# The last expert of a post-norm decoder layer: statistics of the final rows earlier, their normalisation on one engine, one bank per slot tile

## Chip, cores and metric

The kernel runs on one core of one Trainium2 chip. The number judged is the device time of one execution in microseconds. Three runs of the kernel before took 1951.0, 1952.97 and 1957.52 us (median 1952.97).

## What is computed

One decoder layer with layer norm after each of three parts: linear attention, cross attention, and a mixture of experts. Only the third is touched by the change. Cut to that:

```python
logits = xf @ router_w + router_b                 # 2048 tokens, 8 experts
topk_p, topk_i = top_k(softmax(logits), 2)        # two experts per token, weights renormalised
# each expert has cap = 640 slots; tokens are put into slots in order of expert
h  = gelu(einsum('ecd,edf->ecf', buf, w1) + b1[:, None, :])      # 512 -> 1024
eo = einsum('ecf,efd->ecd', h, w2) + b2[:, None, :]              # 1024 -> 512
out = zeros_like(xf).at[st].add(eo_flat[slot] * w)
x = _layernorm(x + out)                            # (x - mean) / sqrt(var + 1e-5), no scale, no shift
```

All is float32. Each large product is made of three products of rounded parts (high x high, high x low, low x high), which is why operands are split into `_hi` and `_lo`.

## The kernel before

The program is one plan, a list of stages written by `do(stage, ...)`; each engine walks the same list and runs the stages that it has a function for. So the order of `do` calls is the order of work on every engine, and an instruction that waits holds all that stands behind it on its engine. Engines hand work over by semaphores (`wait_ge`, `then_inc`); `step.settle` makes VectorE or GpSimd wait for its own last instruction before the next.

Experts go one after another. For expert `e`, `up(e, f)` for f = 0 to 7 computes 128 of the 1024 hidden columns for 640 slots (24 pairs of products of 320 columns on TensorE, line 1440); ScalarE applies the Gelu (line 2077) and makes the high part (line 2082); VectorE makes the low part `hid_lo` (line 1826). A hidden buffer is used by every second f, so the Gelu of f waits for the low part of f - 2. Behind the first four f, ScalarE and VectorE also split the second weights (`split_w2`, line 1821). Then `down(e, i)` for i = 0 to 4 multiplies 128 slots by the second weights (24 products of 512 columns, line 1167, into one PSUM bank). VectorE adds the bias and the router's weight, and GpSimd adds the rows into `y_rows` in HBM, which started as a copy of the input of this part.

The last expert (e = 7) is different. When all rows of the other seven experts lie in `y_rows`, `fetch_y(q)` loads all 2048 rows back in eight pieces of 256 rows (two tiles of 128 each, 512 KB, issued by SyncE), and `gather_y` gathers the 640 rows that belong to the last expert's slots into the five tiles `xg`. Rows without a slot of the last expert are final and only need their layer norm: `final_stats(q)` takes mean and variance on VectorE (line 1869), behind every fourth piece it starts the inverse root, `final_root(half)` ends it on GpSimd with three Newton steps, and the rows are normalised and stored. This is done for all 2048 rows. Rows with a slot of the last expert are done in `finish(7, i)`: product, bias, weight, sum with the gathered row, statistics, inverse root by three Newton steps on one value per partition, normalisation. `scatter` (GpSimd) then writes them over the rows stored before; it waits until all stores of the final rows have landed (`out_done`).

In the kernel before, the eight pieces of final rows are shared: `final_act` takes pieces 0, 1, 4 and 5 on ScalarE, which also issues their stores, `final_dve` takes pieces 2, 3, 6 and 7 on VectorE (line 1885), stored by SyncE. The statistics of pieces 0 to 3 stand behind f = 4 to 7 of the last expert, those of pieces 4 and 5 ahead of `finish(7, 0)` and those of 6 and 7 ahead of `finish(7, 1)`. The products of `finish` use two PSUM banks in turn (6 and 7): TensorE may write a bank again when VectorE has added the bias from it (line 1849).

Of the kernel before, what the change touches and what calls it, by code (L numbers as in the profile page):

```python
# [30 lines left out]
NF = F // P  # L31
# [9 lines left out]
RSQRT_MAGIC = 0x5F3759DF  # L41
PASSES = 3
# [18 lines left out]
HALF_Y = B * NT // 2  # L61

# [63 lines left out]
def program(nc, t):  # L126
    ctx = ExitStack()
    with ctx:
# [183 lines left out]
        def chunk_of(b, mc):  # L312
# [72 lines left out]
        final_act, final_dve = signal("final_act"), signal("final_dve")  # L385
        out_done = signals("out_done", 2, 16)
# [78 lines left out]
            "finish": lambda e, i: (down_summed, eo_biased, slot_ready),  # L465
# [5 lines left out]
            "final_act": lambda q: (final_act, out_done[0]),  # L471
            "final_dve": lambda q: (final_dve, out_done[1]),
# [7 lines left out]
            "fold_turn": folded, "parts": parts_copied, "logits": logits_done, "ranks": ranks_taken, "finish": eo_biased,  # L480
# [563 lines left out]
        def normalise(half):  # L1044
            for q in range(PIECES_Y // 4):
                do("final_act", half * PIECES_Y // 2 + q)
                do("final_dve", half * PIECES_Y // 2 + PIECES_Y // 4 + q)

        for e in range(E):
# [23 lines left out]
            fetch("fetch_w1", e + 2)  # L1073
        for i in range(NS):
            if i < 2:
                for q in range(PIECES_Y // 4):
# [396 lines left out]
        def _(_eng):  # L1473
# [368 lines left out]
            def finish(e, i):  # L1842
                turn = e * NS + i
                out, row, a, b, y = eo[turn % EO], xg[i][:, :], slot_a[:, i:i + 1], slot_b[:, i:i + 1], slot_y[:, i:i + 1]
                dve.wait_ge(*down_summed[e, i])
                dve.wait_ge(*b2_in[e % 2][e])
                if i < EO:
                    dve.wait_ge(*y_added[down_order[turn - EO]])
                V.tensor_tensor(out[:, :], bank(bank_of["finish", e, i]), b2s[e % 2][:, :], ALU.add) \  # L1849
                    .then_inc(eo_biased.sem, 1)  # L1850
                dve.wait_ge(*eo_biased[e, i])
                dve.wait_ge(*xg_in[i][E, i])
# [3 lines left out]
                step.settle(V.tensor_scalar(a, mean_var_s[:, i, 1:2], EPS, None, ALU.add))  # L1856
                step.settle(V.tensor_scalar(y.bitcast(I32), a.bitcast(I32), 1, None, ALU.logical_shift_right))
                step.settle(V.tensor_scalar(y.bitcast(I32), y.bitcast(I32), -1.0, float(RSQRT_MAGIC),
                                            ALU.mult, ALU.add))
# [626 lines left out]
```

## Time and profile before

| | |
|---|---|
| median of 3 runs | 1952.97 us (1951.0 to 1957.52) |
| the profiled execution, its own time | 1955.99 us |
| its span | 1954.2 us, 26706 instructions |
| TensorE / VectorE / ScalarE / GpSimd busy | 97% / 64% / 45% / 42% of the span |
| chain that ended last, by engine | PE 82%, DVE 13%, DMA 2%, the rest 1% or less each |

In the rows below PE is TensorE's matmul, PEld its weight load, DVE is VectorE, ACT is ScalarE, POOL is GpSimd and SP is SyncE; a q behind a name means the queue that issues DMAs. Times are us from the span's start. The chain is followed back from the last instruction, at each step to what released it. A matmul's duration overlaps that of the next one, so their pitch is read from the starts.

### The profile page before, as it was taken

The numbers are of one execution on the slowest core, as the hardware profiler recorded it, in microseconds if no ns is written. First come the engines' busy times: TensorE is split into PE (matmuls) and PEld (weight loads), VectorE is DVE, ScalarE is ACT, GpSimd is POOL, SyncE is SP. The second block draws the span as 40 slices with busy tenths as digits, with TensorE's granted clock in tenths as the row PEclk, the third lists the DMA queues.
The fourth block names the chain that finished last, engine by engine and source line by source line (L and its number), as shares of the span: only waits on it lengthen the run. The fifth ranks groups of instructions, "written<-read, shape, count | busy, mean of one in ns | idle before, by whom it ended". The sixth has DMA issues, their size and how long they took to land.

```text
span 1954.2 us, 26706 instructions
## 1 busy us (share of the span) xinstructions
PE 1886.4 (97%) x10016; PEld 1281.6 (66%) x10016; DVE 1254.8 (64%) x2391; ACT 888.0 (45%) x1595; POOL 822.1 (42%) x740
## 2 busy tenths in 40 slices
PE   8999999989999999999999999999969999999996
PEld 6887677777655555555445545544439998899995
DVE  5675573257778788888678778777653444344457
ACT  3312322222566666666456456546724433344431
POOL 3002201100388788888567657665011223222132
PEclk9999999999999999999999999999978999999998
DMA  7003524573667476757434424421234444434453
GB/s 275 22 1 114 189 87 165 193 208 124 172 132 178 101 182 134 170 120 156 98 103 104 109 59 131 109 65 62 82 111 138 135 125 119 128 99 125 135 140 113
DMA packets 123777, 244.87 MB, mean 125 GB/s; under 512 B 11232, under 2 KB 29424, under 8 KB 119600
## 3 DMA queue, kind: packets, MB, share of 16 engines
q1 hardware_dynamic: 108608, 185.46, 32.0%
q0 software_dynamic: 13952, 55.61, 13.9%
q10 hardware_dynamic: 1088, 2.10, 0.3%
q8 instruction: 79, 1.29, 0.3%
q14 instruction: 50, 0.41, 0.1%
HBM read 148.46 MB, written 62.42 MB: 108 GB/s over the span
## 4 chain that ended last, share of the span: by engine, by line
PE 82%; DVE 13%; DMA 2%; issue 1%; ACT 1%; SPq 1%; POOL 1%; POOLq 0%; DVEq 0%; ACTq 0%
PE banks L1167 34%; PE banks L1440 12%; PE banks L1347 11%; PE banks L1317 10%; PE banks L1336 8%; DVE max L1638 8%; PE banks L1368 4%; PE banks L1173 2%; DMA k_parts<-out_lo 1%; DMA k_half<-in_xwk_t 0%; PE banks L1249 0%; DMA raw<-in_wk_t 0%; DVE stats_y L1869 0%; DVE den_c L1657 0%; POOL x_nat L2148 0%
## 5 line engine op out<-in xcount | busy, mean ns | idle before, releaser
L1638 DVE TENSOR_REDUCE max<-banks 128x1 f32<-128x512 f32 x1024 | 627.1, 680 | 144.3 <-PE banks L1317 143.4
L2137 POOL TENSOR_TENSOR probs<-probs,probs 128x512 f32<-128x512 f32 x464 | 583.0, 1291 | 249.0 <-PE banks L1347 249.0
L2017 ACT ACTIVATE probs<-banks 128x512 f32<-128x512 f32 x1024 | 520.2, 607 | 260.7 <-PE banks L1336 260.1
L1317 PE MATMUL banks<-k_stack,q_stack 98*128 98x512 f32 x1024 | 428.3, 425 | 4.0 <-DVE max L1638 2.7
L1336 PE MATMUL banks<-q_stack,k_stack 98*128 98x512 f32 x1024 | 377.1, 398 | 2.6 <-ACT probs L2017 2.6
L1317 PEld LDWEIGHTS banks<-k_stack,q_stack 98*128 98x128 f32 x1024 | 192.2, 188 | 194.5 <-DVE max L1638 106.2
L1347 PE MATMUL banks<-probs,v_grp 128*32 128x512 f32 x2048 | 251.7, 604 | 0.0
L1336 PEld LDWEIGHTS banks<-q_stack,k_stack 98*128 98x128 f32 x1024 | 191.7, 188 | 62.3 <-ACT probs L2017 17.8
L2184 POOL DMA_INDIRECT y_rows<-eo,tok x35 | 71.4, 2040 | 170.3 <-DVE eo L1839 116.1
L1826 DVE TENSOR_TENSOR hid_lo<-hid,hid_hi 128x640 fp32r<-128x640 f32 x64 | 52.8, 825 | 139.0 <-ACT hid_hi L2082 139.0
L1167 PE MATMUL banks<-w_hi,hid_hi 128*128 128x512 f32 x320 | 129.6, 405 | 2.3 <-DVE eo L1849 2.2
L1347 PEld LDWEIGHTS banks<-probs,v_grp 128*32 128x32 f32 x2048 | 60.2, 109 | 109.1 <-issue 103.0
L2148 POOL TENSOR_TENSOR x_nat<-x_nat,bxo_row 128x512 f32<-128x512 f32 x16 | 21.3, 1360 | 252.3 <-PE banks L1173 252.3
L1167 PE MATMUL banks<-w_hi,hid_lo 128*128 128x512 f32 x320 | 126.8, 396 | 0.0
L1167 PE MATMUL banks<-w_lo,hid_hi 128*128 128x512 f32 x320 | 126.3, 395 | 0.0
L1440 PE MATMUL banks<-xe_hi,w_hi 128*128 128x320 f32 x512 | 117.8, 312 | 1.5 <-issue 1.5
L1440 PE MATMUL banks<-xe_lo,w_hi 128*128 128x320 f32 x512 | 117.8, 311 | 0.0
L1440 PE MATMUL banks<-xe_hi,w_lo 128*128 128x320 f32 x512 | 117.6, 311 | 0.0
L2077 ACT ACTIVATE hid<-banks,b1c 128x640 f32<-128x640 f32 x64 | 51.0, 796 | 137.0 <-PE banks L1440 136.0
L2175 POOL DMA_INDIRECT xg<-x_rows,tok x40 | 39.5, 988 | 167.5 <-PE banks L1173 134.2
L1368 PE MATMUL banks<-probs,ones 128*32 128x512 f32 x784 | 105.7, 601 | 1.5 <-DVE probs L1652 0.8
L1836 DVE TENSOR_TENSOR eo<-banks,b2s 128x512 f32<-128x512 f32 x35 | 24.2, 692 | 106.1 <-PE banks L1167 106.1
(263 smaller groups left out, 2806.7 us busy)
## 6 DMA issues: line engine op xcount, KB each, us to landing
k_stack<-k_parts SPq DMA_DIRECT2D x144, 256.0 KB, 5.3
w_raw<-in_L_ffn_w SPq DMA_DIRECT2D x16, 2048.0 KB, 8.4
probs<-probs POOLq DMA_DIRECT2D x31, 1024.0 KB, 10.1
q_stack<-q_parts SPq DMA_DIRECT2D x48, 256.0 KB
v_grp<-v_rows SPq DMA_DIRECT2D x48, 256.0 KB, 3.3
raw<-in_ctx_t SPq DMA_DIRECT2D x8, 1024.0 KB, 7.1
k_parts<-out_hi SPq DMA_DIRECT2D x32, 256.0 KB, 2.5
k_parts<-out_lo SPq DMA_DIRECT2D x32, 256.0 KB, 2.9
```

The source lines that it names most:

```text
L1167: done = nc.tensor.matmul(out, lhsT, rhs, start=start and n == 0, stop=stop and n == len(operands) - 1)
L1317: nc.tensor.matmul(out, queries_of(t)[:, j, tile_of(k)], keys_of(t)[0:STK + SHIFT, j, mc * HALF:(mc + 1) * HALF], start=True, stop=True) \
L1336: nc.tensor.matmul(out, keys_of(t)[0:STK + SHIFT, j, tile_of(s)], queries_of(t)[:, j, :], start=True, stop=True).then_inc(scored.sem, 1)
L1347: done = nc.tensor.matmul(bank(NUM)[j * DH:(j + 1) * DH, :], v_grp[:, s, j * DH:(j + 1) * DH], probs_of(t, s)[:, j, :], start=s == 0, stop ...
L1368: done = nc.tensor.matmul(bank(DEN)[j * DH:(j + 1) * DH, :], ones[:, 0:DH], tile[:, j, :], start=begun, stop=s == MT - 1 and tile is tiles ...
L1440: done = nc.tensor.matmul(pairs[first][:, h, 0:HC], w, x[:, h * HC:(h + 1) * HC], start=n == 0, stop=n == len(terms) - 1)
L1638: V.reduce_max(max4[:, tiles_of(t), :, :][:, k, j, mc:mc + 1], bank(bank_of["max", t, mc, k, j]), AX.X) \
L1826: V.tensor_tensor(hid_lo[:, f, :], hid[f % 2][:, :], hid_hi[:, f, :].bitcast(F32), ALU.subtract) \
L2017: S.activation(probs_of(t, s)[:, j, :], bank(bank_of["score", t, s, j]), ACT.Exp, scale=SCALE) \
L2077: S.activation(hid[f % 2][:, :].rearrange("p (h n) -> p h n", h=2), pairs[first][:, :, 0:HC], ACT.Gelu, bias=b1c[:, e, f:f + 1]).then_inc( ...
L2137: G.tensor_tensor(a[:, j, :], a[:, j, :], b[:, j, :], ALU.add).then_inc(pair_added.sem, 1)
L2184: G.indirect_dma_start(out=y_rows, in_=eo[turn % EO][:, :], in_offset=None, compute_op=ALU.add, out_offset=bass.IndirectOffsetOnAxis(ap=to ...
```

## The change

`STATS_AT` puts the statistics of the eight pieces behind f = 2 (piece 0), 3 (1), 4 (2, 3), 5 (4, 5) and 6 (6, 7) of the last expert. Both `final_root` and then all eight `final_act` follow the last `up`. `final_dve` is gone: ScalarE normalises all pieces, and SyncE issues all eight stores. The products of the five `finish` stages go to five different banks (6, 7, 4, 5, 0). The bias of the second product is no longer added to the product but to the gathered row, times the slot's weight, in a new stage `bias_slot(i)`, which stands one tile ahead of the `finish` that uses it; so `finish` has one full-width instruction fewer. The Newton iteration of `finish` is written with half the variance, so that a step has two instructions and not three, and one instruction ahead of it falls away (`finish` had 18 instructions and has 13; with `bias_slot` it is 14 per slot tile).

```diff
+HALF_MAGIC = RSQRT_MAGIC - 0x400000 - 2 ** 31
+STATS_AT = {2: (0,), 3: (1,), 4: (2, 3), 5: (4, 5), 6: (6, 7)}
+FINISH_BANKS = (6, 7, 4, 5, 0)
...
-                elif last:
-                    do("final_stats", f - NF // 2)
+                if last:
+                    for q in STATS_AT.get(f, ()):
+                        do("final_stats", q)
             if last:
                 do("final_root", 0)
+                do("final_root", 1)
+                for q in range(PIECES_Y):
+                    do("final_act", q)
                 break
...
+        finish_ring = Ring(*FINISH_BANKS)
+        do("bias_slot", 0)
         for i in range(NS):
-            if i < 2:
-                for q in range(PIECES_Y // 4):
-                    do("final_stats", PIECES_Y // 2 + i * PIECES_Y // 4 + q)
-            if i == 1:
-                do("final_root", 1)
-                normalise(0)
-            if i == 2:
-                normalise(1)
-            do("finish", E - 1, i, ring=down_ring)
+            do("finish", E - 1, i, ring=finish_ring)
+            if i + 1 < NS:
+                do("bias_slot", i + 1)
...
-                V.tensor_tensor(out[:, :], bank(bank_of["finish", e, i]), b2s[e % 2][:, :], ALU.add) \
-                    .then_inc(eo_biased.sem, 1)
-                step.settle(V.scalar_tensor_tensor(row, out[:, :], table[:, 1, turn:turn + 1], row, ALU.mult, ALU.add))
+                step.settle(V.scalar_tensor_tensor(row, bank(bank_of["finish", e, i]), table[:, 1, turn:turn + 1], row,
+                                                   ALU.mult, ALU.add))
...
-                step.settle(V.tensor_scalar(a, a, -0.5, None, ALU.mult))
                 for _ in range(3):
-                    root_step(a, b, y)
+                    step.settle(V.scalar_tensor_tensor(b, y, a, y, ALU.mult, ALU.mult))
+                    step.settle(V.scalar_tensor_tensor(y, b, 1.5, y, ALU.subtract, ALU.mult))
                 V.tensor_scalar(row, row, mean_var_s[:, i, 0:1], y, ALU.subtract, ALU.mult).then_inc(slot_ready.sem, 1)
+            def bias_slot(i):
+                turn = (E - 1) * NS + i
+                row = xg[i][:, :]
+                dve.wait_ge(*b2_in[(E - 1) % 2][E - 1])
+                dve.wait_ge(*xg_in[i][E, i])
+                step.settle(V.scalar_tensor_tensor(row, b2s[(E - 1) % 2][:, :], table[:, 1, turn:turn + 1], row,
+                                                   ALU.mult, ALU.add))
...
-            def final_dve_rows(q):
-                dve.wait_ge(*final_root[q // (PIECES_Y // 2)])
-                for n in range(q * TILES_Y, (q + 1) * TILES_Y):
-                    done = V.tensor_scalar(tile_y(n), tile_y(n), mean_var_y[:, n, 0:1], root_y[:, n:n + 1],
-                                           ALU.subtract, ALU.mult)
-                done.then_inc(final_dve.sem, 1)
...
                 done.then_inc(final_act.sem, 1)
-                act.wait_ge(*final_act[q])
-                S.dma_start(out_rows(q), piece_y(q)).then_inc(out_done[0].sem, 16)
...
-            def final_dve_rows(q):
-                sp.wait_ge(*final_dve[q])
-                Q.dma_start(out_rows(q), piece_y(q)).then_inc(out_done[1].sem, 16)
+            def final_act_rows(q):
+                sp.wait_ge(*final_act[q])
+                Q.dma_start(out_rows(q), piece_y(q)).then_inc(out_done.sem, 16)
```

On VectorE, in the last expert from the low part of f = 2 on, the kernel before has (`hid_lo` is the low part, `w_lo` the split of the second weights, `stats_y` the statistics of a piece, `yf_in0` the landing of piece 0):

```order
L1826 TENSOR_TENSOR hid_lo<-hid_173,hid_hi 128x640 [waits hid_split_hi]
L1821 TENSOR_TENSOR w_lo<-w_raw,w_hi 128x1024 [waits experts_hi]
L1826 TENSOR_TENSOR hid_lo<-hid_174,hid_hi 128x640 [waits hid_split_hi]
L1821 TENSOR_TENSOR w_lo<-w_raw,w_hi 128x1024 [waits experts_hi]
L1826 TENSOR_TENSOR hid_lo<-hid_173,hid_hi 128x640 [waits hid_split_hi]
L1869 BN_STATS stats_y<-y_final_191 128x6 [waits yf_in0]
```

and the changed kernel, from the same low part on:

```order
L1826 TENSOR_TENSOR hid_lo<-hid_173,hid_hi 128x640 [waits hid_split_hi]
L1821 TENSOR_TENSOR w_lo<-w_raw,w_hi 128x1024 [waits experts_hi]
L1871 BN_STATS stats_y<-y_final_191 128x6 [waits yf_in0]
L1871 BN_STATS stats_y<-y_final_191 128x6
L1874 BN_AGGR mean_var_y<-stats_y 128x2 [waits dve_step]
L1874 BN_AGGR mean_var_y<-stats_y 128x2
L1826 TENSOR_TENSOR hid_lo<-hid_174,hid_hi 128x640 [waits hid_split_hi]
L1821 TENSOR_TENSOR w_lo<-w_raw,w_hi 128x1024 [waits experts_hi]
L1871 BN_STATS stats_y<-y_final_191 128x6 [waits yf_in1]
```

The statistics of piece 0 moved from behind the low part of f = 4 to ahead of that of f = 3; the other pieces follow, and all eight stand ahead of the low part of f = 7.

On VectorE, in the last slot tile (i = 4) of the kernel before, with the three Newton steps cut to one:

```order
L1849 TENSOR_TENSOR eo_175<-banks,b2s_179 128x512 [waits down_summed]
L1853 SCALAR_TENSOR_TENSOR xg_168<-eo_175,table,xg_168 128x512 [waits xg_in4,eo_done]
L1854 BN_STATS stats_s<-xg_168 128x6 [waits dve_step]
L1855 BN_AGGR mean_var_s<-stats_s 128x2 [waits dve_step]
L1856 TENSOR_SCALAR slot_a<-mean_var_s 128x1 [waits dve_step]
L1857 TENSOR_SCALAR slot_y<-slot_a 128x1 [waits dve_step]
L1858 TENSOR_SCALAR slot_y<-slot_y 128x1 [waits dve_step]
L1860 TENSOR_SCALAR slot_a<-slot_a 128x1 [waits dve_step]
L1592 TENSOR_TENSOR slot_b<-slot_y 128x1 [waits dve_step]
L1593 TENSOR_TENSOR slot_b<-slot_b,slot_a 128x1 [waits dve_step]
L1594 SCALAR_TENSOR_TENSOR slot_y<-slot_b,slot_y 128x1 [waits dve_step]
```

and of the changed kernel:

```order
L1864 SCALAR_TENSOR_TENSOR xg_168<-b2s_179,table,xg_168 128x512 [waits xg_in4]
L1846 SCALAR_TENSOR_TENSOR xg_168<-banks,table,xg_168 128x512 [waits down_summed,dve_step]
L1848 BN_STATS stats_s<-xg_168 128x6 [waits dve_step]
L1849 BN_AGGR mean_var_s<-stats_s 128x2 [waits dve_step]
L1850 TENSOR_SCALAR slot_a<-mean_var_s 128x1 [waits dve_step]
L1851 TENSOR_SCALAR slot_y<-slot_a 128x1 [waits dve_step]
L1852 TENSOR_SCALAR slot_y<-slot_y 128x1 [waits dve_step]
L1855 SCALAR_TENSOR_TENSOR slot_b<-slot_y,slot_a 128x1 [waits dve_step]
L1856 SCALAR_TENSOR_TENSOR slot_y<-slot_b,slot_y 128x1 [waits dve_step]
```

The wait for the product (`down_summed`) has moved from the first full-width instruction to the second; one full-width instruction is left behind it ahead of the statistics, and a Newton step is two instructions. Between the slot tiles nothing else stands on VectorE any more. TensorE has the same instructions in the same order in both kernels; only the banks of the last three slot tiles differ.

## Rows read from the trace of the kernel before

**Rows 1.** Chain of waits, 1850 to 1955 us: shares by engine and line.
```profile
by line: PE banks L1440 26.8%; PE banks L1167 26.5%; DVE stats_y L1869 5.7%; issue 5.0%; DVE xg L1853 3.6%; DVE stats_s L1854 3.4%; DVE eo L1849 3.1%; DVE y_final L1885 2.9%; DVE slot_b L1593 2.5%; DVE slot_b L1592 2.4%; DVE slot_y L1594 2.
```

**Rows 2.** Windows: stretch, length, busy us of PE, PEld, DVE, ACT, POOL, granted clock, DMA.
```profile
1910.00:1920.00 10.00, 10.00 (x45) 8.15 (x44) 9.20 (x34) 2.35 (x4) 3.71 (x15) 1.00 0.04 14
1920.00:1930.00 10.00, 7.75 (x28) 5.89 (x27) 9.38 (x30) 1.00 (x2) 4.41 (x15) 0.83 0.53 198
```

**Rows 3.** Timeline of PE in the last expert's second products: start, us, what.
```profile
1907.43 0.39 PE L1167 MATMUL banks<-w_hi,hid_hi 128*128 128x512 f32 x1
...
1912.28 0.40 PE L1167 MATMUL banks<-w_hi,hid_hi 128*128 128x512 f32 x1
...
1923.85 0.39 PE L1167 MATMUL banks<-w_hi,hid_lo 128*128 128x512 f32 x1
1926.49 0.80 PE L1167 MATMUL banks<-w_hi,hid_hi 128*128 128x512 f32 x1 [2.25 <-DVE eo L1849]
...
1929.64 0.41 PE L1167 MATMUL banks<-w_lo,hid_hi 128*128 128x512 f32 x1
...
1939.19 0.40 PE L1167 MATMUL banks<-w_hi,hid_lo 128*128 128x512 f32 x1
```

**Rows 4.** Timeline of DVE, the last slot tile.
```profile
1943.87 0.68 DVE L1849 TENSOR_TENSOR eo<-banks,b2s 128x512 f32<-128x512 f32 x1
1944.59 0.75 DVE L1853 SCALAR_TENSOR_TENSOR xg<-eo,table,xg 128x512 f32<-128x512 f32 x1
...
1946.88 0.15 DVE L1860 TENSOR_SCALAR slot_a<-slot_a 128x1 f32<-128x1 f32 x1
1947.07 0.16 DVE L1592 TENSOR_TENSOR slot_b<-slot_y 128x1 f32<-128x1 f32 x1
...
1948.82 0.55 DVE L1863 TENSOR_SCALAR xg<-xg,mean_var_s,slot_y 128x512 f32<-128x512 f32 x1
```

**Rows 5.** Timeline of DVE beside the last expert's first products.
```profile
1891.63 0.82 DVE L1826 TENSOR_TENSOR hid_lo<-hid,hid_hi 128x640 fp32r<-128x640 f32 x1 [1.35 <-ACT hid_hi L2082]
1892.58 1.23 DVE L1821 TENSOR_TENSOR w_lo<-w_raw,w_hi 128x1024 fp32r<-128x1024 f32 x1
1895.15 0.83 DVE L1826 TENSOR_TENSOR hid_lo<-hid,hid_hi 128x640 fp32r<-128x640 f32 x1 [1.35 <-ACT hid_hi L2082]
...
1899.41 1.28 DVE L1869 BATCH_NORM_STATS2 stats_y<-y_final 128x6 f32<-128x512 f32 x2
...
1909.23 0.83 DVE L1826 TENSOR_TENSOR hid_lo<-hid,hid_hi 128x640 fp32r<-128x640 f32 x1 [1.21 <-ACT hid_hi L2082]
1909.97 1.28 DVE L1869 BATCH_NORM_STATS2 stats_y<-y_final 128x6 f32<-128x512 f32 x2
...
1912.06 1.28 DVE L1869 BATCH_NORM_STATS2 stats_y<-y_final 128x6 f32<-128x512 f32 x2
...
1913.54 1.25 DVE L1869 BATCH_NORM_STATS2 stats_y<-y_final 128x6 f32<-128x512 f32 x2
```

**Rows 6.** Issues, 1880 to 1955 (last: landing), and L2420 (fetch of the pieces).
```profile
out<-y_final SPq DMA_DIRECT2D x4, 512.0 KB, 3.4
...
L2420 SPq DMA_DIRECT2D y_final<-y_rows x8: 367/474/1312, 1886.1 to 1889.7; - x8
...
DMA to landing us min/median/max: 5.0/10.8/14.0
```

**Rows 7.** Timeline of POOL: first and last instruction of a root, last scatter.
```profile
1924.10 0.46 POOL L2217 TENSOR_SCALAR final_a<-final_a 128x8 f32<-128x8 f32 x1 [6.99 <-DVE final_y L1879]
...
1929.42 0.24 POOL L2221 TENSOR_SCALAR final_shift<-final_b 128x8 f32<-128x8 f32 x1
...
1950.15 0.97 POOL L2201 DMA_INDIRECT out<-xg,tok  x1 [3.97 <-DVE xg L1863]
```

**Rows 8.** Timeline of ACT: normalisation of one piece.
```profile
1917.15 1.52 ACT L2087 ACTIVATE y_final<-y_final,final_shift,final_y 128x512 f32<-128x512 f32 x2 [7.95 <-POOL final_shift L2221]
```

More of the change, by code:

```diff
@@ L384, in program @@
         final_stats, final_root = signal("final_stats"), signal("final_root")
-        final_act, final_dve = signal("final_act"), signal("final_dve")
-        out_done = signals("out_done", 2, 16)
+        final_act = signal("final_act")
+        out_done = signal("out_done", 16)
         dve_step, pool_step = (ctx.enter_context(nc.semaphore(n)) for n in ("dve_step", "pool_step"))
@@ L464, in program @@
             "down": lambda e, i: (down_summed, eo_biased, eo_ready, y_added),
-            "finish": lambda e, i: (down_summed, eo_biased, slot_ready),
+            "finish": lambda e, i: (down_summed, slot_ready),
             "scatter": lambda e, i: (slot_out,),
@@ L470, in program @@
             "final_root": lambda half: (final_root,),
-            "final_act": lambda q: (final_act, out_done[0]),
-            "final_dve": lambda q: (final_dve, out_done[1]),
+            "final_act": lambda q: (final_act, out_done),
         }
@@ L479, in program @@
             "score": exp_done, "num": num_copied, "den": den_copied, "rows": xo_added, "fold": fold_copied,
[L480 removed]
+            "fold_turn": folded, "parts": parts_copied, "logits": logits_done, "ranks": ranks_taken, "finish": slot_ready,
             "table": table_added, "x1_logits": part_hi, "turn_xe": xe_split, "up": hid_done, "down": eo_biased,
@@ L1843, in finish @@
                 turn = e * NS + i
-                out, row, a, b, y = eo[turn % EO], xg[i][:, :], slot_a[:, i:i + 1], slot_b[:, i:i + 1], slot_y[:, i:i + 1]
+                row, a, b, y = xg[i][:, :], slot_a[:, i:i + 1], slot_b[:, i:i + 1], slot_y[:, i:i + 1]
                 dve.wait_ge(*down_summed[e, i])
-                dve.wait_ge(*b2_in[e % 2][e])
-                if i < EO:
-                    dve.wait_ge(*y_added[down_order[turn - EO]])
-                V.tensor_tensor(out[:, :], bank(bank_of["finish", e, i]), b2s[e % 2][:, :], ALU.add) \
-                    .then_inc(eo_biased.sem, 1)
@@ L1851, in finish @@
-                dve.wait_ge(*eo_biased[e, i])
-                dve.wait_ge(*xg_in[i][E, i])
-                step.settle(V.scalar_tensor_tensor(row, out[:, :], table[:, 1, turn:turn + 1], row, ALU.mult, ALU.add))
+                step.settle(V.scalar_tensor_tensor(row, bank(bank_of["finish", e, i]), table[:, 1, turn:turn + 1], row,
+                                                   ALU.mult, ALU.add))
                 step.settle(V.bn_stats(stats_s[:, i, :], row))
                 step.settle(V.bn_aggr(mean_var_s[:, i, :], stats_s[:, i, :]))
-                step.settle(V.tensor_scalar(a, mean_var_s[:, i, 1:2], EPS, None, ALU.add))
+                step.settle(V.tensor_scalar(a, mean_var_s[:, i, 1:2], EPS, 0.5, ALU.add, ALU.mult))
@@ L1857, in finish @@
                 step.settle(V.tensor_scalar(y.bitcast(I32), a.bitcast(I32), 1, None, ALU.logical_shift_right))
-                step.settle(V.tensor_scalar(y.bitcast(I32), y.bitcast(I32), -1.0, float(RSQRT_MAGIC),
+                step.settle(V.tensor_scalar(y.bitcast(I32), y.bitcast(I32), -1.0, float(HALF_MAGIC),
                                             ALU.mult, ALU.add))
-                step.settle(V.tensor_scalar(a, a, -0.5, None, ALU.mult))
                 for _ in range(3):
-                    root_step(a, b, y)
+                    step.settle(V.scalar_tensor_tensor(b, y, a, y, ALU.mult, ALU.mult))
+                    step.settle(V.scalar_tensor_tensor(y, b, 1.5, y, ALU.subtract, ALU.mult))
@@ L1898, in _ @@
                     "turn_xe": turn_xe, "split_w1": split_w1, "split_w2": split_w2, "up": up,
-                    "down": down, "finish": finish, "final_stats": final_statistics, "final_dve": final_dve_rows}
+                    "down": down, "finish": finish, "bias_slot": bias_slot, "final_stats": final_statistics}
             for stage, *key in plan:
@@ L2102, in _ @@
                     here[stage](*key)
-            act.wait_ge(*out_done[0].now())
         @block.gpsimd
@@ L2198, in scatter @@
                 pool.wait_ge(*slot_ready[e, i])
-                for x in out_done:
-                    pool.wait_ge(*x.now())
+                pool.wait_ge(*out_done.now())
                 G.indirect_dma_start(out=all_out_rows, in_=xg[i][:, :], in_offset=None,
@@ L2433, in _ @@
                     "store_x2": store_x2, "fetch_w1": fetch_w1, "fetch_w2": fetch_w2, "fetch_b1": fetch_b1,
-                    "fetch_b2": fetch_b2, "fetch_y": fetch_y, "final_dve": final_dve_rows}
+                    "fetch_b2": fetch_b2, "fetch_y": fetch_y, "final_act": final_act_rows}
             for stage, *key in plan:
@@ L2437, in _ @@
                     here[stage](*key)
-            sp.wait_ge(*out_done[1].now())
+            sp.wait_ge(*out_done.now())
 def kernel(**inputs):
```

4 lines of the change are left out of this document (removed).

## The prediction

> **What bounds the kernel now.** First the chain of waits over the last 105 us [rows 1]: the products of the last two experts lead it, and behind them come only VectorE lines (statistics of the final rows L1869, the slot tiles L1853, L1854, L1849, the final rows L1885, the Newton steps). So the chain changes hands from TensorE to VectorE in the last expert. Next the windows [rows 2]: from 1910 to 1930 VectorE is busy 9.20 and 9.38 us of 10, while TensorE falls from 10.00 to 7.75 with the granted clock at 0.83. Then TensorE's timeline [rows 3]: the second products of the last expert start at 1907.43, run without a break to 1923.85, and then stop 2.25 us for VectorE's bias addition L1849, which frees the bank; the last of the 120 starts at 1939.19. VectorE's timeline [rows 4] ends at 1948.82 + 0.55 = 1949.37, 9.8 us behind TensorE's end (1939.59). The last scatter starts at 1950.15 [rows 7] and the span ends at 1954.2. So the end is set by VectorE's queue, filled from 1912.06 on with statistics and final rows between the slot tiles. The rest of the program, some 1885 us, is not touched.
>
> **Step 1, TensorE without its stop.** With five banks none is used twice, so no product waits for a bias addition. 72 products took 1923.85 + 0.23 - 1907.43 = 16.65 us [rows 3], 5.55 per slot tile and 0.231 each. All 120 from 1907.43: the last starts at 1907.43 + 119 x 0.231 = 1934.95 and ends 0.40 later, at 1935.35. Before, it ended at 1939.59, so TensorE gets back 4.24 us; the chain does not see this until VectorE is fast enough.
>
> **Step 2, the statistics under the first products.** What must hold: VectorE's low part of f = 7 must be done when TensorE comes to its first product of f = 7, the 22nd, at 1912.28 [rows 3]. Prices [rows 5]: a low part 0.74 to the next start (1909.23 to 1909.97; 0.83 if it is waited for), a split of weights 1.23, a piece of statistics 1.48 (1912.06 to 1913.54), a piece with a root's start behind it 2.09 (1909.97 to 1912.06). The ups come every 3.52 us (1891.63, 1895.15).
> - f = 2: the split ends at 1892.58 + 1.23 = 1893.81, piece 0 at 1895.29; the low part of f = 3 was due at 1895.15, so 0.14 late.
> - f = 3: the split still waits for ScalarE (1892.58 + 3.52 = 1896.10) and ends at 1897.33, piece 1 at 1898.81; the next low part was due at 1898.67.
> - f = 4: low part to 1899.55, two pieces and a root's start, 3.57, to 1903.12 (due 1902.19).
> - f = 5: low part and two pieces, 3.70, to 1906.82 (due 1905.71).
> - f = 6: low part, two pieces, a root's start, 4.31, to 1911.13 (due 1909.23).
> - f = 7: the low part ends at 1911.13 + 0.83 = 1911.96.
>
> That is 1.90 us later than before and still 0.32 us ahead of 1912.28. The Gelu of f waits for the low part of f - 2, which was due two ups, 7.04 us, ahead of that of f; for f - 2 = 5 and less it is at most 1.0 us late, so no first product moves. The cost on the path is 0, from 0 to 1 us: it is 0.5 if each of the eight pieces costs 0.1 more than its row, and 1 with 0.16. I take 0. The pieces must also have landed. They took 5.0 to 14.0 us to land from issue [rows 6], were issued from 1886.1 to 1889.7, and land in order of issue as I read the spread; then piece 0 lies there at about 1891, needed at 1893.81, and piece 7 at 1903.7, needed at about 1909.1.
>
> **Step 3, a slot tile's own length.** From the first instruction that reads the bank. Before: 1943.87 to 1949.37, 5.50 us. Now: the weighted sum to the end of the last preparation, 1946.88 - 1944.59 = 2.29; six small instructions for nine, 6 x (1948.82 - 1947.07)/9 = 1.17; the normalisation 0.55; 4.01 us in all [rows 4]. The bias for the next tile is one instruction like L1853, 0.78 with its gap. Together 4.79, under TensorE's 5.55 per tile. So VectorE waits for TensorE in every tile, and the five banks matter only together with this. `bias_slot(0)` runs from 1911.96 to 1912.74, before the first sum ends at 1913.1.
>
> A price that the rows do not show is the weighted sum read from PSUM (L1853 read SBUF alone, 0.75). Rows bound it: a sum of 640 columns from SBUF takes 0.83 and 1024 columns 1.23 [rows 5], which makes 0.69 for 512, and L1849 with PSUM takes 0.68 [rows 4]. So PSUM costs nothing here that can be seen; I take 0.75, from 0.68 to 0.85. The Trainium skill (VectorE: DVE Perf Modes, section on the TRN2 errata) gives PSUM sources a fixed cost 62 cycles higher than SBUF sources, 0.065 us as an estimate; by it the end comes 0.07 us later. The measured pair above disagrees, and I go by the rows.
>
> **Step 4, the end.** The last sum is there at 1935.35, plus 0.04 for the handover (estimate; 0 to 0.1), plus 4.01: 1939.40. Before it was 1949.37. From there to the end of the span it was 4.83 us (scatter, landing), which stays, since `scatter(4)` has nothing ahead of it: the span ends at 1944.23.
>
> **Step 5, what could make the scatters late.** They wait for all stores of final rows. GpSimd's first root starts at 1903.1 and takes 5.56 us at most (1924.10 to 1929.66) [rows 7], the second starts at 1911.1 and ends at 1916.7. ScalarE is free at 1909.2 and needs 1.52 us per piece [rows 8]: pieces 0 to 3 to 1915.3, pieces 4 to 7 from 1916.7 to 1922.8. A store lands 3.4 us after issue [rows 6]; with SyncE's start, all have landed at about 1927. The first slot tiles are ready before, tile 2 at 1928.2, so scatters 0 to 2 run from 1927 to 1931, tile 3's at 1934.5, tile 4's at 1940.2. ScalarE may be 8 us late before anything moves. Taking four pieces from VectorE thus costs nothing; the cover is ScalarE's idle time. The stores move from ScalarE's queue to SyncE's, which has nothing else left.
>
> **Sum.** 1949.37 - 1939.40 = 9.97 us. The profiled execution took 1955.99, 1.8 over its span; it would take 1946.0. It was 3.0 us slower than the median of the runs, so from the median 1952.97 - 9.97 = **1943.0 us**, -0.5%. Own range of this case: 1941.0 to 1945.5, from step 2 (up to 1 us later), the PSUM read (-0.1 to +0.1) and the scatter of runs (1951.0 to 1957.5 before).
>
> **Rivals.**
> - *A, the low part of f = 7 comes late.* For it: only 0.32 us of room behind eight pieces and two root starts without one idle gap from f = 4 on. Against it: every price is from a row of the same instructions. If each piece costs 0.25 more, the seven from f = 3 on make 1.75, less 0.32 of room: 1.4 us of stop in slot tile 0, all later tiles shift by it, 1944.4. After the stop of 2.25 us seven products took 1929.64 - 1926.49 = 3.15 us [rows 3] where 7 x 0.231 = 1.62 is the rule; 1.5 more for that clock: 1945.9.
> - *B, the statistics wait for their pieces.* For it: piece 0 is now wanted 5.6 us earlier than its first use at 1899.41 [rows 5], and 14.0 us is a landing that occurred [rows 6]. If that were piece 0's, it would land at 1900.1, 6.3 late; the queue behind it is full, so the low part of f = 7 would be some 6.3 late, less 0.3 of room, and 1.5 for the clock: gain 2.5, 1950.5. Against it: the shortest landing is 5.0, and pieces issued first should be the short ones.
> - *C, slower than before: the stop comes together with a clock that stays low.* In the stop of A or B the granted clock falls from 2.4 to 1.2 GHz, as after the stop of 2.25 us (0.83 in that stretch [rows 2], products 0.45 apart [rows 3]), and here it would have to stay there. Behind the 22nd product 99 are left; at 0.22 us more each they cost 21.8 us against a gain of 9.97 less a stop of 1 us: 1965.8. It decides from about 41 products at the low level, where before there were seven. For it: only that the fall exists. Against it: after the stop in the rows the products were at full pitch again within 3.2 us. The Trainium skill (TensorE: Matmul & The Clock Gate, section on HAM oscillation) tells of kernels in which each wait brings the low clock back again. By that rule the removed stop would be a gain of its own, and one that step 1 already holds.
> - *D, the change does not shorten the end:* VectorE is still the bound because the slot tile did not shrink below TensorE's 5.55. It would need 0.76 us more in 14 instructions. With 6.0 us per tile in place of 4.79, and the last without a bias behind it, the end is 1913.1 + 4 x 6.0 + 5.2 = 1942.3 for 1939.4, time 1945.9.
>
> **Chances.** My forecast 0.74, A 0.12, B 0.05, C 0.02, D 0.03; 0.04 for effects elsewhere in the program, of either sign. A measurement of this kernel tells about 0.3%, 5.9 us, from no change: "faster" means below 1947.1. The forecast, A and D lie below it (0.89), but their runs scatter by some 3 us, so faster 0.86; B and part of the rest are within 0.3%: 0.11; C and the rest slower: 0.03. The range for 8 in 10 reaches from 1939.5 to 1947.5: it holds the forecast with the scatter of runs, A and D, not B or C.
>
> **What the profile after would show.** Right: products of the last expert's second stage at 0.231 apart from 1907.4 to 1935 with no gap, granted clock 1.00 from 1920 to 1930; a wait for TensorE ahead of the weighted sum in each slot tile, about 0.7 us; the tile 4.0 us long; VectorE's last instruction ending at 1939.4; the last scatter at about 1940.2. Wrong: a gap on TensorE ahead of the 22nd product; idle time of VectorE ahead of statistics, put down to a DMA; a low part of f = 7 ending after 1912.3; scatters that start later than their tiles by more than 1 us, put down to stores. My prediction fails if VectorE's end moves by less than 6 us, or if TensorE's start at 1907.43 moves.

## The result and the profile after

Ten runs of the changed kernel have a median of 1943.69 us (1940.12 to 1950.17), ten of the kernel before one of 1956.66 us (1951.0 to 1961.13). The ratio is 0.9936, 95% interval 0.992 to 0.9953: 9 to 16 us less. The prediction was 1943.0 us and a gain of 9.97 us, which is a ratio of 0.9949. The profiled execution took 1940.12 us with a span of 1938.3, which is 15.9 us less than the span before. This is more than the forecast, and the first question is where it lies.

The measure used from here on is the **tail**: from the start of the first of the 120 last products to the end of VectorE's last instruction. Before it is 1949.37 - 1907.43 = 41.94 us [rows 3, 4]. Of the changed kernel, the timeline of TensorE:

```profile
1901.30 0.39 PE L1167 MATMUL banks<-w_hi,hid_hi 128*128 128x512 f32 x1
...
1906.15 0.40 PE L1167 MATMUL banks<-w_hi,hid_hi 128*128 128x512 f32 x1
...
1928.81 0.39 PE L1167 MATMUL banks<-w_hi,hid_lo 128*128 128x512 f32 x1
```

and of VectorE (the low part of f = 7, then slot tile 0, then the last slot tile):

```profile
1904.80 0.82 DVE L1826 TENSOR_TENSOR hid_lo<-hid,hid_hi 128x640 fp32r<-128x640 f32 x1
1905.54 0.75 DVE L1864 SCALAR_TENSOR_TENSOR xg<-b2s,table,xg 128x512 f32<-128x512 f32 x1
1907.13 0.75 DVE L1846 SCALAR_TENSOR_TENSOR xg<-banks,table,xg 128x512 f32<-128x512 f32 x1 [0.85 <-PE banks L1167]
...
1929.31 0.75 DVE L1846 SCALAR_TENSOR_TENSOR xg<-banks,table,xg 128x512 f32<-128x512 f32 x1 [0.69 <-PE banks L1167]
1930.09 0.69 DVE L1848 BATCH_NORM_STATS2 stats_s<-xg 128x6 f32<-128x512 f32 x1
...
1931.61 0.22 DVE L1855 SCALAR_TENSOR_TENSOR slot_b<-slot_y,slot_a 128x1 f32<-128x1 f32 x1
1931.86 0.16 DVE L1856 SCALAR_TENSOR_TENSOR slot_y<-slot_b,slot_y 128x1 f32<-128x1 f32 x1
1932.06 0.22 DVE L1855 SCALAR_TENSOR_TENSOR slot_b<-slot_y,slot_a 128x1 f32<-128x1 f32 x1
...
1932.95 0.55 DVE L1857 TENSOR_SCALAR xg<-xg,mean_var_s,slot_y 128x512 f32<-128x512 f32 x1
```

The tail is 1933.50 - 1901.30 = **32.20 us, 9.74 less** (predicted 9.97). Three things stand in these rows. TensorE has no stop: the 120 products start within 27.51 us. VectorE waits for TensorE ahead of the weighted sum, 0.85 us in the first tile and 0.69 in the last; in the kernel before it came to the last tile without a wait [rows 4]. And the low part of f = 7 ends at 1905.62, 0.53 us ahead of the 22nd product at 1906.15.

The windows of the changed kernel over the same stretch of work answer to [rows 2]; TensorE is busy throughout, at full granted clock (columns: stretch, length, busy us of PE, PEld, DVE, ACT, POOL, then granted clock and DMA):

```profile
1903.90:1913.90 10.00, 10.00 (x45) 8.15 (x44) 7.90 (x24) 8.53 (x13) 4.03 (x15) 1.00 0.69 258
1913.90:1923.90 10.00, 10.00 (x45) 8.12 (x44) 7.88 (x28) 2.05 (x3) 2.08 (x2) 1.00 0.50 189
```

VectorE fell from 9.2 to 7.9 us in 10. ScalarE's two groups of final rows and GpSimd's scatters, again of the changed kernel:

```profile
1902.97 5.75 ACT L2082 ACTIVATE y_final<-y_final,final_shift,final_y 128x512 f32<-128x512 f32 x8
1910.19 5.76 ACT L2082 ACTIVATE y_final<-y_final,final_shift,final_y 128x512 f32<-128x512 f32 x8 [1.47 <-POOL final_shift L2212]
```
```profile
1921.51 1.09 POOL L2192 DMA_INDIRECT out<-xg,tok  x1 [11.36 <-DMA out<-y_final]
...
1928.87 0.97 POOL L2192 DMA_INDIRECT out<-xg,tok  x1 [3.56 <-DVE xg L1857]
1934.29 0.97 POOL L2192 DMA_INDIRECT out<-xg,tok  x1 [4.45 <-DVE xg L1857]
```

ScalarE is done with all rows at 1915.95; the first scatter waits for the stores until 20.2 us behind the first product, but the last two wait only for their own tiles. From VectorE's end to the end of the span it is 4.8 us, as before.

So the tail gives 9.74 of the 15.9 us, and 6.13 us lie ahead of it (1907.43 to 1901.30), in code that is the same in both kernels. The windows say where. Before:

```profile
400.00:450.00 50.00, 43.59 (x175) 33.97 (x173) 29.98 (x50) 10.29 (x18) 0.00 (x0) 0.93 0.66 192
...
1300.00:1350.00 50.00, 47.41 (x278) 23.89 (x282) 38.56 (x95) 28.88 (x57) 32.16 (x28) 0.96 0.30 89
1350.00:1400.00 50.00, 50.00 (x308) 23.50 (x300) 35.13 (x53) 38.34 (x78) 12.89 (x16) 0.97 0.25 85
```

and after:

```profile
400.00:450.00 50.00, 44.00 (x188) 34.70 (x188) 32.28 (x53) 10.28 (x18) 0.00 (x0) 1.00 0.70 203
...
1300.00:1350.00 50.00, 47.43 (x279) 24.89 (x272) 40.68 (x99) 30.64 (x61) 35.40 (x31) 1.00 0.27 79
1350.00:1400.00 50.00, 50.00 (x318) 23.23 (x317) 36.55 (x52) 39.00 (x79) 9.07 (x13) 1.00 0.25 85
```

TensorE's granted clock was 0.93 to 0.97 in these three stretches before and 1.00 after. Whether that belongs to the change is taken up by the last experiments.

### The profile page after: what moved, and what is told of

It reads as the page before. It is cut to its first block, busy times and chain, and to the rows that moved or that the text cites. A ratio compares the mean times of both kernels' runs of the same rounds, so it can differ in the third digit from the quotient of the medians.

```text
span 1938.3 us, 26683 instructions
## 1 busy us (share of the span) xinstructions
PE 1878.2 (97%) x10016; PEld 1277.8 (66%) x10016; DVE 1249.2 (64%) x2363; ACT 893.1 (46%) x1603; POOL 821.2 (42%) x740
## 4 chain that ended last, share of the span: by engine, by line
PE 83%; DVE 11%; DMA 2%; issue 1%; SPq 1%; ACT 1%; POOL 1%; POOLq 0%; DVEq 0%; ACTq 0%
PE banks L1167 35%; PE banks L1440 12%; PE banks L1347 11%; PE banks L1317 10%; PE banks L1336 9%; DVE max L1638 8%; PE banks L1368 4%; PE banks L1173 2%; DMA k_parts<-out_lo 1%; DMA k_half<-in_xwk_t 0%; PE banks L1249 0%; DMA raw<-in_wk_t 0%; DVE den_c L1657 0%; POOL x_nat L2140 0%; PE banks L1325 0%
```

## The experiments

The tail of each kernel is read from one trace. Only e11 and e12 were also timed over several executions. "First product" is the start of the 120; times are us, and the last column is the tail less that of the changed kernel.

| | first product at | last product, from it | tail | against changed |
|---|---|---|---|---|
| before | 1907.43 | 31.76 | 41.94 | +9.74 |
| changed | 1901.30 | 27.51 | 32.20 | |
| e1 two banks | 1903.91 | 27.51 | 32.20 | 0.00 |
| e2 banks only | 1907.22 | 27.51 | 41.94 | +9.74 |
| e3 early statistics only | 1904.68 | 27.51 | 36.69 | +4.49 |
| e4 late statistics | 1907.32 | 27.51 | 35.85 | +3.65 |
| e5 old slot tile | 1904.63 | 27.51 | 33.44 | +1.24 |
| e6 rows back on VectorE | 1902.00 | 27.51 | 33.26 | +1.06 |
| e7 statistics crowded | 1900.72 | 28.58 | 33.27 | +1.07 |
| e8 more crowded | 1906.66 | 31.54 | 36.23 | +4.03 |
| e9 piece 0 sooner | 1904.99 | 27.51 | 32.20 | 0.00 |
| e10 two Newton steps | 1903.96 | 27.51 | 31.76 | -0.44 |
| e11 before again | 1904.29 | 31.76 | 41.91 | +9.71 |
| e12 two steps, timed | 1906.42 | 27.51 | 31.75 | -0.45 |

**e1, two banks again.**
```diff
-FINISH_BANKS = (6, 7, 4, 5, 0)
+FINISH_BANKS = (6, 7)
```


> The changed kernel with the slot tiles' products in two banks (6, 7) again. Measure: the tail, from the start of the first of the last 120 products to the end of VectorE's last instruction (before 41.94 us, changed kernel 32.20). Theory 1 (a bank is read by one instruction right behind its sum, and is wanted again only 5.5 us later): tail 32.2 +- 0.1, no gap on TensorE. Theory 2 (the five banks are a part of the gain, as the stop of 2.25 us before suggests): tail 33 to 36.5, a gap on TensorE ahead of the fourth slot tile.

Measured: tail 32.20, no gap on TensorE. VectorE's last instruction of slot tile 0, TensorE's first product of tile 2 (which wants the bank of tile 0 again) and VectorE's weighted sum of tile 1:

```profile
1913.40 0.55 DVE L1857 TENSOR_SCALAR xg<-xg,mean_var_s,slot_y 128x512 f32<-128x512 f32 x1
1915.01 0.39 PE L1167 MATMUL banks<-w_hi,hid_hi 128*128 128x512 f32 x1
1915.28 0.75 DVE L1846 SCALAR_TENSOR_TENSOR xg<-banks,table,xg 128x512 f32<-128x512 f32 x1 [0.67 <-PE banks L1167]
```

The bank is read by one instruction of 0.75 us, but that is not when TensorE gets it back, as the expectation has it. The change also moved the signal that frees a bank: in the kernel before it is given by the bias addition (`eo_biased`), in the changed kernel and in e1 by the last instruction of the slot tile (`slot_ready`). So the bank is free at 1913.95 and wanted at 1915.01, which leaves 1.06 us of room. That is enough: with the rest of the change, the five banks are worth nothing. I had written that they "matter only together with this"; they do not matter even then. Whether a tile that is late by more than this 1.06 us would make two banks stop TensorE was not tried.

**e2, five banks in the kernel before.**
```diff
+        finish_ring = Ring(6, 7, 4, 5, 0)
...
-            do("finish", E - 1, i, ring=down_ring)
+            do("finish", E - 1, i, ring=finish_ring)
```


> The kernel before with five banks and nothing else of the change. Theory 1 (VectorE's queue sets the end, TensorE's stop costs nothing): tail 41.9 +- 0.2, while TensorE's last product starts 4.2 us earlier, 27.5 us behind the first. Theory 2 (TensorE's stop is on the path): tail 38 to 40.

Measured, by the first and last product of the 120 and VectorE's last instruction:

```profile
1907.22 0.39 PE L1168 MATMUL banks<-w_hi,hid_hi 128*128 128x512 f32 x1
1934.73 0.39 PE L1168 MATMUL banks<-w_hi,hid_lo 128*128 128x512 f32 x1
1948.61 0.55 DVE L1864 TENSOR_SCALAR xg<-xg,mean_var_s,slot_y 128x512 f32<-128x512 f32 x1
```

TensorE's last product starts 27.51 us behind the first, not 31.76, and the tail is 41.94 as before. TensorE's stop of 2.25 us, the most visible thing in [rows 3], was off the path.

**e3, only the early statistics and roots.**
```diff
-                elif last:
-                    do("final_stats", f - NF // 2)
+                if last:
+                    for q in {2: (0,), 3: (1,), 4: (2, 3), 5: (4, 5), 6: (6, 7)}.get(f, ()):
+                        do("final_stats", q)
...
                 do("final_root", 0)
+                do("final_root", 1)
...
-            if i < 2:
-                for q in range(PIECES_Y // 4):
-                    do("final_stats", PIECES_Y // 2 + i * PIECES_Y // 4 + q)
             if i == 1:
-                do("final_root", 1)
```


> The kernel before with the statistics and roots placed as in the changed kernel, all else as before (two banks, old slot tile, four pieces of final rows on VectorE). Theory 1 (sum of VectorE's queue behind the first sum: 5 x 5.46 for the tiles and 2 x 1.83 for the rows, begun at 5.6 us): tail 36.6, a gain of 5.3 of the 9.7 us. Theory 2 (the statistics only move the load: the low part of f = 7 comes late and TensorE stops): a gap on TensorE ahead of the 22nd product, tail over 38.

Measured, again by first product, last product and VectorE's last instruction:

```profile
1904.68 0.39 PE L1165 MATMUL banks<-w_hi,hid_hi 128*128 128x512 f32 x1
1932.19 0.39 PE L1165 MATMUL banks<-w_hi,hid_lo 128*128 128x512 f32 x1
1940.82 0.55 DVE L1861 TENSOR_SCALAR xg<-xg,mean_var_s,slot_y 128x512 f32<-128x512 f32 x1
```

The tail is 36.69, a gain of 5.25 alone. With two banks and the old slot tile TensorE has no stop any more (27.51): the stop needed both the statistics in VectorE's queue and only two banks.

**e4, the changed kernel with the statistics late.**
```diff
-STATS_AT = {2: (0,), 3: (1,), 4: (2, 3), 5: (4, 5), 6: (6, 7)}
+STATS_AT = {4: (0,), 5: (1,), 6: (2,), 7: (3,)}
...
-                do("final_root", 1)
-                for q in range(PIECES_Y):
+                for q in range(PIECES_Y // 2):
                     do("final_act", q)
...
+            if i < 2:
+                for q in range(PIECES_Y // 4):
+                    do("final_stats", PIECES_Y // 2 + i * PIECES_Y // 4 + q)
+            if i == 1:
+                do("final_root", 1)
+                for q in range(PIECES_Y // 2, PIECES_Y):
+                    do("final_act", q)
```


> The changed kernel with the statistics and the second root placed as in the kernel before. Theory 1 (VectorE's queue is the bound again: 7.5 us to the end of piece 5's statistics, five tiles of 4.9, two pieces and a root's start 3.6): tail 35.5 to 36, +3.3 to +3.8 over the changed kernel. Theory 2 (the slack in each tile takes the statistics in): tail 32.2 to 33.5.

Measured: 35.85, as theory 1 has it. And one more thing: from VectorE's end (1943.17) to the end of the span it is 5.4 us, 0.6 more than elsewhere. GpSimd's timeline shows why:

```profile
1939.26 1.07 POOL L2198 DMA_INDIRECT out<-xg,tok  x1 [10.15 <-DMA out<-y_final]
1940.63 1.01 POOL L2198 DMA_INDIRECT out<-xg,tok  x1 [0.30 <-issue]
1941.95 0.97 POOL L2198 DMA_INDIRECT out<-xg,tok  x1 [0.30 <-issue]
1943.23 0.97 POOL L2198 DMA_INDIRECT out<-xg,tok  x1 [0.30 <-DVE xg L1863]
1944.51 0.97 POOL L2198 DMA_INDIRECT out<-xg,tok  x1 [0.30 <-issue]
```

The final rows land late, all five scatters stand in a queue at 1.3 us each, and the last starts 1.34 us behind its tile, not 0.79. In the changed kernel that queue has run empty 4.5 us before its last scatter. The early statistics keep two bounds off, not one.

**e5, the old slot tile** (bias on the product, three-instruction Newton step, no `bias_slot`).
```diff
-                step.settle(V.scalar_tensor_tensor(row, bank(bank_of["finish", e, i]), table[:, 1, turn:turn + 1], row,
-                                                   ALU.mult, ALU.add))
...
+                V.tensor_tensor(out[:, :], bank(bank_of["finish", e, i]), b2s[e % 2][:, :], ALU.add) \
+                    .then_inc(eo_biased.sem, 1)
...
+                step.settle(V.scalar_tensor_tensor(row, out[:, :], table[:, 1, turn:turn + 1], row, ALU.mult, ALU.add))
...
                 for _ in range(3):
+                    root_step(a, b, y)
```


> The changed kernel with the slot tile of the kernel before: bias added to the product, long Newton step, no separate bias stage. Theory 1 (a tile of 5.46 us is still just under TensorE's 5.55, so only the last one counts, 5.50 for 4.19 us): tail 33.5, +1.3. Theory 2 (VectorE falls behind in every tile): tail over 35.

Measured: 33.44. The first instruction of the tiles starts every 5.54 to 5.55 us, TensorE's own pace:

```profile
1915.93 0.69 DVE L1846 TENSOR_TENSOR eo<-banks,b2s 128x512 f32<-128x512 f32 x1
...
1921.47 0.69 DVE L1846 TENSOR_TENSOR eo<-banks,b2s 128x512 f32<-128x512 f32 x1
```

So a tile of 5.5 us just keeps up, and shortening it pays once, in the last tile.

**e6, four pieces of final rows back on VectorE.**
```diff
         for i in range(NS):
+            if i in (1, 2):
+                normalise(i - 1)
             do("finish", E - 1, i, ring=finish_ring)
```
`normalise(half)` is that of the kernel before: of each half, two pieces on ScalarE, which stores them itself, and two on VectorE. The eight `final_act` behind the last `up` are gone.

> The changed kernel with pieces 2, 3, 6 and 7 of the final rows normalised by VectorE again, ahead of slot tiles 1 and 2, and ScalarE storing its own. Theory 1 (each group of 1.83 us stands in a slack of 0.63 us per tile, and what is left over is worked off by the later tiles): tail 33.3, +1.1 (0.9 to 1.4). Theory 2 (VectorE's slack hides the rows): +0 to +0.3. Theory 3 (all of it counts): +3.6.

Measured: 33.26. The two groups of 1.83 us stand on VectorE; the slack of the tiles (0.62 to 0.69 us in each tile from the second on in the changed kernel) takes in 2.6 us of 3.66, and the rest, 1.06 us, is what the last tile starts late.

**e7 and e8, statistics crowded towards the end.** Rival A made real.
```diff
-STATS_AT = {2: (0,), 3: (1,), 4: (2, 3), 5: (4, 5), 6: (6, 7)}
+STATS_AT = {3: (0,), 4: (1, 2), 5: (3, 4), 6: (5, 6, 7)}        # e7
+STATS_AT = {4: (0, 1), 5: (2, 3), 6: (4, 5, 6, 7)}              # e8
```


> The changed kernel with pieces 0 to 7 of the statistics behind f = 3, 4, 4, 5, 5, 6, 6, 6, so that the low part of f = 7 comes about 1.6 us later than in the changed kernel and ends 1.1 us behind the moment that TensorE wants it. Rival A of the prediction made real. Theory 1: TensorE stops 1.1 us ahead of the 22nd product, tail 33.3, granted clock unchanged. Theory 2: the clock falls too and comes back as after the stop of 2.25 us before, tail 34.8. Theory 3 (rival C): it stays at the lower level, tail over 50.

> The same with pieces behind f = 4, 4, 5, 5, 6, 6, 6, 6: the low part of f = 7 ends 2.5 us behind its moment. Theory 1: stop of 2.5 us, tail 34.7, clock unchanged. Theory 2: the clock falls for some seven products, tail 36.2. Theory 3 (rival C): it stays low, tail over 50.

TensorE of e7, with the 22nd product:

```profile
1906.54 0.50 PE L1167 MATMUL banks<-w_hi,hid_hi 128*128 128x512 f32 x1 [0.81 <-DVE hid_lo L1826]
1906.87 0.40 PE L1167 MATMUL banks<-w_lo,hid_hi 128*128 128x512 f32 x1
```

and of e8:

```profile
1913.87 0.50 PE L1167 MATMUL banks<-w_hi,hid_hi 128*128 128x512 f32 x1 [2.20 <-DVE hid_lo L1826]
...
1914.93 0.63 PE L1167 MATMUL banks<-w_hi,hid_hi 128*128 128x512 f32 x1
...
1917.49 0.53 PE L1167 MATMUL banks<-w_hi,hid_hi 128*128 128x512 f32 x1
1917.85 0.39 PE L1167 MATMUL banks<-w_lo,hid_hi 128*128 128x512 f32 x1
```

e7: the low part ends 5.76 us behind the first product, the stop costs 1.07 and nothing else. e8: it ends at 7.16, the stop costs 2.4, and then products are 0.43 us apart (1914.50 to 1917.49), 1.7 us more than at full clock; the tail grows by 4.03, and all later tiles shift by it. The clock was back after 3.6 us, with 89 products to go. Rival C, the clock that stays low, is refuted for stops of up to 2.2 us.

**e9, piece 0 two places nearer to its landing.**
```diff
-STATS_AT = {2: (0,), 3: (1,), 4: (2, 3), 5: (4, 5), 6: (6, 7)}
+STATS_AT = {1: (0,), 2: (1,), 3: (2,), 4: (3,), 5: (4, 5), 6: (6, 7)}
```


> The changed kernel with piece 0 behind f = 1, piece 1 behind f = 2, pieces 2 and 3 behind f = 3 and 4. It measures when piece 0 lands (rival B): VectorE comes to it 4.0 us behind its issue. Theory 1 (pieces land in the order of issue, the first within 5 us): VectorE waits 0 to 1 us for a DMA, the low part of f = 7 is earlier than in the changed kernel, tail 32.2. Theory 2 (a late landing of 10 to 14 us can be piece 0's): VectorE waits 6 to 10 us, and the tail grows to 36 to 40.

Measured: no wait, tail 32.20. VectorE takes piece 0 at 1887.77, 4.25 us behind its issue at 1883.52 (columns: durations ns, first and last start):

```profile
L2411 SPq DMA_DIRECT2D y_final<-y_rows x8: 367/471/1254, 1883.5 to 1887.2; - x8
...
DMA to landing us min/median/max: 4.1/9.2/14.2
```
```profile
1887.77 1.28 DVE L1871 BATCH_NORM_STATS2 stats_y<-y_final 128x6 f32<-128x512 f32 x2
```

So the short landing is piece 0's, as read, and rival B was far off: in the changed kernel piece 0 is wanted 7.45 us behind its issue (1880.14 to 1887.59), where e9 has it landed within 4.25. The row of these loads in the changed kernel's own trace gives 7.4 us as the shortest landing, but that is the third piece's; the trace lacks the landings of the first two.

**e10, two Newton steps.** Each of the new steps turns the sign of y, and the start value is negative so that three steps end positive. With two the rows come out with the wrong sign, and less exact.
```diff
-                for _ in range(3):
+                for _ in range(2):
```


> The changed kernel with two Newton steps in place of three for the slot tiles; the root is less exact. Theory 1 (the last tile's chain is serial up to the end): tail 31.74, 0.46 shorter (two instructions, 0.45 us per step after the traces). Theory 2 (something else than VectorE ends the tile): 32.2.

Measured: 31.76. The last chain is serial: a step of 0.45 us taken from it makes the tail 0.44 us shorter.

**e11, the kernel before once more, timed against itself.** No edit.

> The kernel before once more, timed against itself. The profiled pair differed by 15.9 us in span, of which the tail makes 9.74; 6.13 us lie ahead of the first of the 120 products. Theory 1 (this is scatter between executions, in stretches of other granted clock): the start of the 120 products lies anywhere from 1900 to 1908, tail 41.9, ratio 1.000 within 0.2%. Theory 2 (the changed kernel is faster ahead of the tail too): the start lies at 1907 again, and all runs of the changed kernel's kind start at about 1901.

Measured: ratio 0.9998 (0.9984 to 1.0012), tail 41.91, first product at 1904.29, 3.1 us earlier than in the first trace of the same kernel. Over the 14 traces it lies anywhere from 1900.72 to 1907.43, with kernels of the old and of the new kind mixed: e2, which is the kernel before but for banks, at 1907.22, but e4 and e8, variants of the changed kernel, at 1907.32 and 1906.66. So most of the 6.13 us ahead of the tail can be had without the change, as scatter between executions: the kernel before against itself moved by 3.1 us, and the changed kernel's kind reaches nearly as late as the latest of the old kind. In TensorE's timelines of the first pair the 6.13 us come in two steps, of about 3 us around 400 us and about 3 us around 1350 us; from 1600 us up to the first product nothing is added.

In this second trace TensorE has a second stop, of 1.44 us, ahead of slot tile 4, and no low clock. In the first trace it has the low clock behind the first stop and next to no second one. Slot tile 4 starts 26.3 us and the last product 31.76 us behind the first product in both. What the clock took was time that TensorE would have waited for VectorE anyway, which is e2's finding once more.

**e12, two steps with the right sign, timed.**
```diff
-HALF_MAGIC = RSQRT_MAGIC - 0x400000 - 2 ** 31
+HALF_MAGIC = RSQRT_MAGIC - 0x400000
...
-                for _ in range(3):
+                for _ in range(2):
```


> The changed kernel with two Newton steps for the slot tiles and a start value of the other sign, so that the root is positive after two steps; its relative error is about 5e-6 in place of rounding. It is the candidate that beats both kernels. Theory 1 (the tail is serial and nothing else is on it): tail 31.76 as with the other two-step kernel, 10.2 us less than before, ratio to the kernel before 0.9948, within 0.993 to 0.997. Theory 2 (the changed kernel is also 2 to 3 us faster ahead of the tail, as the medians of its ten runs suggest): ratio 0.9930 or less.

Measured: tail 31.75, 10.19 less than before; ratio to the kernel before 0.9946 (0.9927 to 0.9965), median 1940.48 against 1950.81 us. Expected 0.9948. Its tail is the shortest of all; against the changed kernel that is 0.45 us, which no comparison of whole times here could tell.

## Why the prediction was right

**What bounds.** Right, and it is the step on which all rests. VectorE's queue set the end; e2 gave TensorE its 4.25 us back and moved nothing.

**Step 1.** Predicted 1934.95 - 1907.43 = 27.52 us from first to last product, measured 27.51. But the cause was named too kindly to the banks: in e1 and e3 two banks never stop TensorE, once the statistics are out of VectorE's queue.

**Step 2.** The low part of f = 7 was forecast to end 4.53 us behind the first product, with 0.32 us of room; it ended at 4.32, with 0.53. The price of a piece, 1.48 us, held. e7 shows that the room was real and small: 1.44 us later, and TensorE stops. The landings were read rightly from minimum and maximum (e9).

**Step 3.** The term that was mis-sized, by 0.25 of 9.97 us. The forecast took 4.01 us from the first reader of the bank and 0.04 for the handover; measured 4.19 and 0.11 (1928.81 + 0.39 = 1929.20 to 1929.31). The 0.18 are the three L1855: I had priced the new two-tensor instruction with a scalar from memory like the nine old ones, 0.194 us from start to start, and it takes 0.25 (0.22 busy where L1592 to L1594 take 0.16). No run separates the scalar from memory from the rest of that instruction; L1856, of the same kind with an immediate scalar, takes 0.16. So the step of two instructions costs 0.45 us and not 0.39; the old one of three cost 0.58. The weighted sum from PSUM takes 0.75 us, the same as L1864 with all in SBUF: the rows were right. The Trainium skill (VectorE: DVE Perf Modes, section on the TRN2 errata) gives PSUM sources a fixed cost 62 cycles higher than SBUF sources. In this instruction the trace shows no such difference, 0.75 against 0.75 us.

**Step 4.** From VectorE's end to the end of the span 4.8 us, forecast 4.83.

**Step 5.** The first scatter, which waits for the stores, started 20.2 us behind the first product, forecast 19.6. Two errors partly cancel: ScalarE took 1.44 us per piece, forecast 1.52, and the slowest store took 4.6 us to land, where the forecast took the median of 3.4. The cover was there, and e4 shows what is behind it when it is gone.

**The sum, and how it divides.** 9.97 forecast, 9.74 measured. From the kernel before, the early statistics alone bring 5.25 us (e3); the other 4.49 come from rows on ScalarE and the shorter tile together. Taken out of the changed kernel one by one, the statistics cost 3.65, the tile 1.24, the rows 1.06 and the banks 0.00, together 5.95: less than 9.74, because with one of them gone the tiles' slack still takes up part of it, and with all gone there is no slack.

**The whole time.** 1943.0 forecast, 1943.69 measured, but that both agree so well is luck in part: the base moved from 1952.97 (three runs) to 1956.66 (ten), so the measured difference is 13 us and not 10. The ratio is the fair comparison: 9.74 us of 1956.66 is 0.9950, inside the interval of 0.992 to 0.9953 but at its edge. The ten runs of the kernel before seem to have been high: when it was timed again beside the experiments, its medians were 1952.83 (17 runs), 1952.73 (12) and 1950.81 (9), while e1 and e9, which have the changed kernel's tail, took 1942.75 and 1943.82 in one run each. e12 with five runs gave 0.9946 where the tail says 0.9948. That the changed kernel might be faster ahead of the tail too is not ruled out for an us or more, since the starts of its kind reach down to 1900.72 and those of the old kind only to 1904.29; four traces of the old kind are too few to tell, and nothing in the code speaks for it.

**The rivals.** A did not happen. Made real, it behaved as described, but its two prices did not come together for short stops: in e8 stop and clock cost 2.4 + 1.7 us, in e7 the stop alone, 1.07, and in e11 a stop of 1.44 us, the size that A named, kept the full clock. A's 1.5 us for the clock is thus not shown for a stop of its size. B was refuted by e9, C by e8. D did not happen: a tile took 5.55 us with 0.6 to 0.7 of it waiting.

## What to carry to other kernels

Where an engine's queue sets the end, add up what stands in that queue behind the last hand-over, and move out what does not need to be there; the stop that one sees on the other engine may be only its shadow, and taking it away (here with more banks) brings nothing. As soon as VectorE's work on a slot tile is shorter than TensorE's, shortening it pays once, in the last tile, and no longer five times (e5: 1.24 us in all). And measure such an end from a mark inside the trace: between two marks two traces of the same kernel agreed to 0.03 us (41.94 and 41.91), while the whole times leave 3 us to either side.

## What the runs showed of the hardware

- After the same stop of TensorE (2.25 us, for L1849) the granted clock fell in the first trace of the kernel before [rows 3] and did not in the second, where the next products start 0.34 and then 0.23 us apart:

```profile
1923.35 0.50 PE L1167 MATMUL banks<-w_hi,hid_hi 128*128 128x512 f32 x1 [2.25 <-DVE eo L1849]
1923.69 0.39 PE L1167 MATMUL banks<-w_lo,hid_hi 128*128 128x512 f32 x1
1923.92 0.39 PE L1167 MATMUL banks<-w_hi,hid_lo 128*128 128x512 f32 x1
```

  The 3.15 us behind the stop, by windows of the first trace and of the second, and the 3.15 us behind the second trace's stop of 1.44 us (columns as in [rows 2]):

```profile
1926.49:1929.64 3.15, 3.15 (x7) 2.48 (x8) 2.81 (x11) 0.00 (x0) 2.40 (x10) 0.50 0.68 256
1923.35:1926.50 3.15, 3.15 (x14) 2.58 (x15) 2.81 (x11) 0.00 (x0) 2.41 (x9) 1.00 0.68 256
1930.62:1933.77 3.15, 3.15 (x14) 2.57 (x15) 2.81 (x11) 0.00 (x0) 0.00 (x0) 1.00 1.01 378
```

  Of three stops of 2.20 to 2.25 us (these two and e8's) two were followed by the low level; the stops of 1.44 us here and of 0.81 us in e7 were not. The tail is the same in both traces, since it was VectorE's.
- The start of the last 120 products, behind 1900 us of the same work, scatters over 6.7 us. Where the clock was low differs from trace to trace: in the first pair around 400 and 1300 to 1400 us, but e2, which starts at 1907.22, has 1.00 in all three of those stretches and 0.97 from 200 to 300 us, where the changed kernel has 1.00. What decides on it was not found.
- A `scalar_tensor_tensor` of one column with its scalar in memory and two tensor inputs takes 0.22 us (L1855), one with an immediate scalar 0.16 (L1856).
